# First attention: value matmuls in bursts of four units instead of two, eight probability buffers instead of six, and a shorter scope for a projection table

## The chip, the cores and the metric

The kernel runs on one core of one Trainium2 chip. The metric is the device time of one execution in microseconds; three runs of the kernel before gave 4062.64, 4070.68 and 4073.54 us, a median of 4070.68 us. PE is the matmul engine, DVE VectorE, ACT ScalarE, POOL GpSimd, and SP issues DMAs.

## The reference

The program is a stack of four blocks with a layer norm behind each. Only the first is touched:

```python
q = (x @ Wq.T + bq).reshape(B, T, H, hd)      # B 2, T 2048, H 16, hd 16
k = (x @ Wk.T + bk).reshape(B, T, H, hd)
v = (x @ Wv.T + bv).reshape(B, T, H, hd)
scores = jnp.einsum('bqhd,bkhd->bhqk', q, k) * scale
lag = jnp.abs(idx[:, None] - idx[None, :]).astype(jnp.float32)
scores = scores * jnp.exp(-alpha * lag)
attn = jax.nn.softmax(scores, axis=-1)
out = jnp.einsum('bhqk,bkhd->bqhd', attn, v).reshape(B, T, D)
return out @ Wo.T + bo
```

Behind it come a feed-forward with weights and activations quantized to four bits, a linear attention and a mixture of eight experts.

## The kernel before

**Units and tiles.** The heads are taken two at a time, 16 pairs in all (2 batches times 8). For each pair the scores are computed twice. The first time, 128 "tiles" of 128x512 serve only to find the maximum of every query's row: PE computes a tile into one of three PSUM buffers (`ps_r`, `BANKS = 3`, L623), DVE multiplies it by the decay and takes its maximum in one instruction, followed by a short one that reads the result (both L690), and the buffer is free again. The second time, 64 "units" of 128 keys x 512 queries x 2 heads make the output: PE computes a unit's scores with two matmuls into one of two PSUM buffers (`ps_s`, L645), ACT takes their exp into `prob` (L779), and PE multiplies the probabilities by the values (L661) into `ps_o`. A unit's values are four matmuls in float32, on four strips of 32 columns of the array, which the trace records as eight.

**Diagonal units.** Where keys and queries lie in the same 512 columns (16 of 64 units) the decay can't be folded into the operands. ACT copies such scores to `tb` (L769), POOL multiplies by the decay and subtracts the maxima (L737, L740), and ACT takes the exp from there (L776). `SCORE_ORDER` and `EXP_ORDER` say in which order the 16 units of a block of 512 queries are scored and exponentiated; a diagonal unit's exp comes several units after its copy.

**Order of the work.** It is written out by hand in `body_steps`. A body runs a pair's 64 units beside the tiles of the pair behind it (102 of them, and the first 26 of the one after), two tiles to a unit. `values` steps are put behind every second unit, and cover the two units that lie `LAG` = 4 back. Once in 16 units a `sum` step transposes the finished output (L668), which ACT has moved from `ps_o` to `ot` before (L756, behind the second exp of the next block, when the last values of the block are done), and DVE divides by the sums (L718, L720). The last pair's body has no tiles; the one before it has 102. The middle bodies stand in a loop of two pairs per turn.

**Waits.** PE's tile waits for `ring_free`, which DVE raises when it has read the tile that was in the buffer; its score n waits until ACT has read n-2; its values wait for the exps. An exp n waits for `value`, that is until the values of the unit that last used the same of the `RING` = 6 probability buffers are computed. `PV0` is the count from which `value` starts, one below `RING`.

**The projection table.** `grow` (4 KB a partition), `nalpha`, `alpha` and three bias columns are written by `stage_tables` and read by `stage_project`, both of which are over when `stage_attention` opens; they are held in SBUF until the attention ends.

Of the kernel before, what the change touches and what calls it, by code (L numbers as in the profile page):

```python
# [14 lines left out]
P = 128  # L15
B, T, D = 2, 2048, 256
N = B * T
KC = D // P
NT = N // P
TB = T // P  # L20
# [3 lines left out]
CH = 512  # L24
QB = T // CH
# [32 lines left out]
def up_to(n):  # L58

    return n + 1  # L60
# [257 lines left out]
UNITS = QB * TB  # L318
# [4 lines left out]
TURN = 3  # L323
BANKS = 3
EARLY = 3
RING = 6
LAG = 4
EXP0, PV0, EV0 = TB, 5, 1

# [45 lines left out]
@lru_cache(None)  # L377
def body_steps(kind):

    fold, turn = [("fold", None, 1)], [("turn", None, 1)]
    if kind == "first":
        small = [("tile", t, 1) for t in range(TILES)] + fold + [("tile", t, 2) for t in range(TURN)] + turn
        small += [("tile", t, 2) for t in range(TURN, SKEW)]
        steps, slot = [], 0
        for what, n, ahead in small:
            steps.append((what, n, slot if what != "fold" else None, ahead))
            slot += what != "fold"
        return steps  # L390
    small = []
    if kind != "last":
        small = [("tile", t, 1) for t in range(SKEW, TILES)] + fold
        if kind in ("lead", "mid"):
            small += [("tile", t, 2) for t in range(TURN)] + turn + [("tile", t, 2) for t in range(TURN, SKEW)]
        else:
            small += turn
    steps, done, slot = [], 0, 0
    def next_small(upto):
        nonlocal done, slot  # L400
        while done < min(len(small), upto):
            what, n, ahead = small[done]
            steps.append((what, n, slot if what != "fold" else None, ahead))
            done, slot = done + 1, slot + (what != "fold")

    for two in range(0, UNITS + (LAG if kind == "last" else 0), 2):
        for u in (two, two + 1):
            next_small(EARLY + 2 * u)
            if u < UNITS:
                steps.append(("score", u, None, 0))  # L410
            next_small(EARLY + 2 * u + 1)
        if two >= LAG:
            steps.append(("values", two - LAG, None, 0))
        elif kind != "lead":
            steps.append(("values", UNITS + two - LAG, None, -1))
        if two % TB == TB // 2 and (two > TB or kind != "lead"):
            steps.append(("sum", two // TB - 1 if two > TB else QB - 1, slot, 0 if two > TB else -1))
            slot += 1
    assert done == len(small)
    if kind == "last":  # L420
        steps.append(("sum", QB - 1, slot, 0))
    return steps
# [30 lines left out]
def stage_attention(nc, g, a):  # L453
    with ExitStack() as ctx:
# [61 lines left out]
        with nc.Block() as block:  # L516
# [89 lines left out]
            @block.tensor  # L606
            def _(pe):
                def body(_, this, nxt):
                    for kind, n, slot, ahead in body_steps(body_kind(this, nxt)):
                        whose = (this or nxt.plus(-1)).plus(ahead)  # L610
                        if slot is not None:
                            bank, back = ring_use(body_kind(this, nxt))[slot]
                            at_slot = first_slot(this) + slot
                            if this or slot >= BANKS:

                                pe.wait_ge(s["ring_free"], up_to(at_slot - back + 1))
                        if kind == "tile":
                            hh, rest = divmod(n, TB * QB)
                            qt, kc = divmod(rest, QB)
                            if n == 0:  # L620
                                pe.wait_ge(s[f"p1load{whose.par}"], up_to(whose.half() * 192 + 192))
                            buf = p1[whose.par]
                            pe.matmul(ps_r[:, bank, :], buf[:, hh, 0, qt * P:(qt + 1) * P],  # L623
                                      buf[:, hh, 1, kc * CH:(kc + 1) * CH], start=True, stop=True)\
                              .then_inc(s["ring_full"], 1)
                        elif kind == "turn":
                            pe.wait_ge(s["mred"], up_to(nxt.times(1) + 1))
                            pe.transpose(ps_r[0:2 * TB, bank, 0:P], nm[:], ident[:]).then_inc(s["ring_full"], 1)
                        elif kind == "score":
                            qb, kb, diag = s_unit(n)  # L630
                            if n == 0:
                                pe.wait_ge(s[f"p2load{this.par}"], up_to(this.half() * 288 + 288))
                            if n == 1:
                                pe.wait_ge(s[f"mload{this.par}"], up_to(this.half() * 128 + 128))
                            if SCORE_ORDER[(n - 2) % TB] == "d":

                                pe.wait_ge(s["copied"], up_to(this.times(TB) + diag_count(n - 2) + 1))
                            else:

                                pe.wait_ge(s["exp"], up_to(this.times(UNITS) + place_in(SCORE_ORDER, n - 2, EXP_ORDER) + 1 + EXP0))  # L640
                            buf = p2[this.par]
                            rows = ROWS if diag else ROWS + AUG
                            var = RAW if diag else LEFT if kb < TPC * qb else RIGHT
                            for hh in range(2):
                                mm = pe.matmul(ps_s[:, n % 2, hh, :], buf[0:rows, hh, KEY, kb * P:(kb + 1) * P],  # L645
                                               buf[0:rows, hh, var, qb * CH:(qb + 1) * CH], start=True, stop=True)
                            mm.then_inc(s["score"], 1)
                        elif kind == "values":
                            if n == 0:
                                pe.wait_ge(s[f"vload{whose.par}"], up_to(whose.half() * 16 + 16))  # L650
                            if n % TB == 0:

                                pe.wait_ge(s["evac"], up_to(whose.times(QB) + n // TB + EV0))
                            pe.wait_ge(s["exp"], up_to(whose.times(UNITS) + n + 2 + EXP0))
                            for m in (n, n + 1):
                                qb, kb, _ = e_unit(m)
                                for f in range(2):
                                    for hh in range(2):
                                        q = 2 * f + hh
                                        out = ps_o[32 * q:32 * q + VW, qb % 2, :]  # L660
                                        mm = pe.matmul(out.rearrange("p (j c) -> p j c", c=P), vp[whose.par][:, kb, hh, :],  # L661
                                                       prob[:, m % RING, hh, :].rearrange("p (j f c) -> p f j c", f=2, c=P)[:, f],
                                                       start=(m % TB == 0), stop=(m % TB == TB - 1), skip_group_check=True)
                                mm.then_inc(s["value"], 1)
                        elif kind == "sum":
                            pe.wait_ge(s["evac"], up_to(whose.times(QB) + n + 1 + EV0))
                            for j in range(2):
                                mm = pe.transpose(ps_r[:, bank, j * P:(j + 1) * P], ot[:, j * P:(j + 1) * P], ident[:])  # L668
                            mm.then_inc(s["ring_full"], 1)

                walk(body)(pe)
# [74 lines left out]
            def _(act):  # L746
                def body(_, this, nxt):
# [11 lines left out]
                    for n in range(UNITS):  # L759
# [8 lines left out]
                                act.wait_ge(s["exp"], up_to(this.times(UNITS) + place_in(SCORE_ORDER, mine - 1, EXP_ORDER) - TB + 1 + EXP0))  # L768
                                act.activation(tb[:, k % DIAGS], ps_s[:, (mine - 1) % 2], ACT.Copy).then_inc(s["copied"], 1)  # L769

                        last = UNITS % RING if n < UNITS % RING else RING
                        act.wait_ge(s["value"], up_to(this.times(UNITS) + n - last + 1 + PV0))
                        if diag:
                            k = e_diags.index(n)
                            act.wait_ge(s["less"], up_to(this.times(TB) + k + 1))
# [1397 lines left out]
def post_ln_stack(nc, inputs, out):  # L2173
# [3 lines left out]
    with ExitStack() as ctx:  # L2177
        g = {}

        def sbuf(where, name, shape, dt=F32):  # L2180
            g[name] = where.enter_context(nc.sbuf_tensor(name, shape, dt))
# [14 lines left out]
        sbuf(ctx, "ident", [P, P])  # L2196
        with ExitStack() as attention:
            sbuf(attention, "toep", [P, TOEP])
            sbuf(attention, "grow", [P, 2, CH])
            sbuf(attention, "csc", [P, QB * TB])  # L2200
            sbuf(attention, "nalpha", [P, 1])
            sbuf(attention, "alpha", [P, 1])
            for n in ("bq", "bk", "bq4"):
                sbuf(attention, n, [P, KC])
            stage_tables(nc, g, a)
            stage_project(nc, g, a)
            stage_attention(nc, g, a)
        sbuf(ctx, "logit", [P, NT, E])
        sbuf(ctx, "gate", [P, 2, NT])
# [50 lines left out]
```

## Time and profile before

| | us |
|---|---|
| median of three runs | 4070.68 (4062.64 to 4073.54) |
| the profiled execution, its own time | 4065.74 |
| its span | 4064.2 |
| PE busy | 3197.6 (79%) |
| DVE busy | 2557.4 (63%) |
| ACT busy | 1755.8 (43%) |
| POOL busy | 1472.8 (36%) |

The shares are averages over stages with different limits. The first attention lies between about 300 and 1953 us of the span. Times of rows are counted from the span's start. A row of the timeline gives the start, how long it lasted, the engine, the line and what was computed, merged over instructions of one kind that follow one another (x16), and in brackets an idle stretch before it with what ended it. A matmul's time in a row includes the way through the array; how fast matmuls follow one another is read from their starts.

### The profile page before, as it was taken

What the parts mean: (1) busy time and instruction counts of PE and PEld (TensorE: products, weight loads), DVE (VectorE), ACT (ScalarE), POOL (GpSimd) and SP (SyncE); (2) the same over time, 40 slices, a digit from 0 to 9 for tenths busy, and PEclk for the clock granted to TensorE, in tenths of its full rate; (3) what the DMA queues carried; (4) which work ended last, traced back from release to release, by engine and by line L of the source; (5) the groups of instructions that cost most, each with busy time, mean ns of one, the idle gap of its engine ahead of it and who ended that gap; (6) DMA issues with size and microseconds to landing.
All of it is one profiled execution on the core that took longest, in us unless ns stands there. A gap on an engine that the chain in (4) does not pass through costs nothing. (4 is left out here: it accounts for less than half of the span.)

```text
span 4064.2 us, 72075 instructions
## 1 busy us (share of the span) xinstructions
PE 3197.6 (79%) x21589; PEld 1637.2 (40%) x21590; DVE 2557.4 (63%) x6592; ACT 1755.8 (43%) x2093; POOL 1472.8 (36%) x811
## 2 busy tenths in 40 slices
PE   5539999999999989998335887788887339999970
PEld 2202333333333333332123454455565216666650
DVE  6739998989898989991476777354444302222226
ACT  3302887878787878889211222111211102222210
POOL 2212777777777777778100000000000230000016
PEclk8756999999999999999667999899997569999985
DMA  4743333333333333330230000110001550000014
GB/s 112 216 113 75 82 84 81 75 82 76 81 76 80 77 80 77 79 62 26 50 61 16 11 15 0 71 41 29 25 22 78 206 201 31 31 31 31 31 47 143
DMA packets 200466, 285.30 MB, mean 70 GB/s; under 512 B 91760, under 2 KB 156272, under 8 KB 197840
## 3 DMA queue, kind: packets, MB, share of 16 engines
q1 hardware_dynamic: 185968, 234.81, 23.0%
q0 software_dynamic: 13312, 43.30, 3.0%
q8 instruction: 172, 2.82, 0.3%
q10 hardware_dynamic: 864, 3.15, 0.2%
q14 instruction: 150, 1.23, 0.1%
HBM read 185.37 MB, written 79.00 MB: 65 GB/s over the span
## 5 line engine op out<-in xcount | busy, mean ns | idle before, releaser
L690 DVE CUSTOM_DVE_ANT_0 ps_r<-ps_r,toep 128x512 f32<-128x512 f32 x2048 | 1356.2, 717 | 194.8 <-PE ps_r L623 137.6
L779 ACT ACTIVATE prob<-ps_s,csc 128x1024 f32<-128x1024 f32 x768 | 836.7, 1119 | 185.1 <-PE ps_s L645 134.6
L623 PE MATMUL ps_r<-p 96*128 96x512 bf16 x2048 | 746.4, 403 | 130.9 <-DMA p<-scr_scratch 78.7
L737 POOL TENSOR_TENSOR tb<-tb,toep 128x1024 f32<-128x1024 f32 x256 | 606.1, 2367 | 484.7 <-ACT tb L769 336.6
L645 PE MATMUL ps_s<-p 120*128 120x512 bf16 (+1 forms) x2048 | 618.2, 384 | 41.9 <-ACT tb L769 26.6
L740 POOL TENSOR_TENSOR tb<-tb,mb 128x1024 f32<-128x1024 f32 x256 | 605.6, 2366 | 20.1
L661 PE MATMUL ps_o<-prob,vp 128*32 128x256 f32 x8192 | 553.1, 388 | 1.0 <-ACT prob L779 1.0
L623 PEld LDWEIGHTS ps_r<-p 96*128 96x128 bf16 x2048 | 199.1, 98 | 601.5 <-DVE mp L690 323.8
L769 ACT ACTIVATE tb<-ps_s 128x1024 f32<-128x1024 f32 x256 | 263.0, 1027 | 202.2 <-PE ps_s L645 202.1
L661 PEld LDWEIGHTS ps_o<-prob,vp 128*32 128x32 f32 x8192 | 214.8, 109 | 280.1 <-issue 190.7
L645 PEld LDWEIGHTS ps_s<-p 120*128 120x128 bf16 (+1 forms) x2048 | 181.6, 99 | 273.2 <-ACT prob L779 70.5
L690 DVE DVE_READ_ACCUMULATOR2_ANT mp<- 128x1 f32 x2048 | 290.4, 142 | 0.0
L2014 PE MATMUL ps_ed<-moe_w,e_aT 128*128 x1152 | 267.5, 385 | 16.9 <-ACT e_aT L2034 16.9
L2034 ACT ACTIVATE e_aT<-ps_et 128x512 f32<-128x512 f32 x144 | 78.2, 595 | 461.7 <-PE ps_et L2006 461.7
L776 ACT ACTIVATE prob<-tb 128x1024 f32<-128x1024 f32 x256 | 270.9, 1058 | 3.6 <-POOL tb L740 3.6
L1986 PE MATMUL ps_eu<-moe_w,e_hT 128*128 x584 | 267.1, 601 | 3.1 <-DVE e_hT L2050 3.1
L2014 PEld LDWEIGHTS ps_ed<-moe_w,e_aT 128*128 128x128 f32 x1152 | 212.9, 190 | 59.6 <-issue 33.6
L2059 DVE TENSOR_TENSOR e_u<-ps_eu,moe_b 128x1024 f32<-128x1024 f32 x73 | 89.4, 1225 | 225.5 <-PE ps_eu L1986 225.5
L2103 POOL MEMSET c_acc<- 1x1 f32 x1 | 0.1, 88 | 630.1 <-POOLq L48 630.1
L2073 DVE TENSOR_TENSOR e_y<-ps_ed,moe_b 128x256 f32<-128x256 f32 x72 | 30.6, 425 | 229.5 <-PE ps_ed L2014 229.5
L1127 PE MATMUL ps_u<-wgu,xs 128*128 128x512 f32 (+1 forms) x384 | 161.6, 571 | 6.9 <-DMA xs<-xqT 6.9
L1986 PEld LDWEIGHTS ps_eu<-moe_w,e_hT 128*128 128x128 f32 x584 | 112.4, 193 | 114.9 <-issue 111.3
(289 smaller groups left out, 3540.2 us busy)
## 6 DMA issues: line engine op xcount, KB each, us to landing
p<-scr_scratch SPq DMA_DIRECT2D x288, 192.0 KB
mb<-mrow_scratch SPq DMA_DIRECT2D x16, 2048.0 KB, 7.1
scr_scratch<-part SPq DMA_DIRECT2D x64, 384.0 KB, 6.1
moe_w<-in_W_dram SPq DMA_DIRECT2D x16, 1024.0 KB
p<-scr_scratch SPq DMA_DIRECT2D x96, 128.0 KB
slots_scratch<-l_zero POOLq DMA_DIRECT2D x16, 592.0 KB, 5.2
e_xs<-slots_scratch SPq DMA_DIRECT2D x74, 128.0 KB, 2.0
yslots_scratch<-e_y SPq DMA_DIRECT2D x72, 128.0 KB, 1.7
```

The source lines that it names most:

```text
L623: pe.matmul(ps_r[:, bank, :], buf[:, hh, 0, qt * P:(qt + 1) * P], buf[:, hh, 1, kc * CH:(kc + 1) * CH], start=True, stop=True)\
L645: mm = pe.matmul(ps_s[:, n % 2, hh, :], buf[0:rows, hh, KEY, kb * P:(kb + 1) * P], buf[0:rows, hh, var, qb * CH:(qb + 1) * CH], start=True ...
L661: mm = pe.matmul(out.rearrange("p (j c) -> p j c", c=P), vp[whose.par][:, kb, hh, :], prob[:, m % RING, hh, :].rearrange("p (j f c) -> p f ...
L690: dve.tensor_tensor_reduce(ps_r[:, bank, :], ps_r[:, bank, :], toep[:, col:col + CH], 1.0, -3.0e38, ALU.mult, ALU.max, mp[:, whose.par, hh ...
L737: pool.tensor_tensor(tb[:, k % DIAGS], tb[:, k % DIAGS], toep[:, col:col + CH].unsqueeze(1) .broadcast_to([P, 2, CH]), ALU.mult).then_inc( ...
L740: pool.tensor_tensor(tb[:, k % DIAGS], tb[:, k % DIAGS], mb[:, this.par, :, qb * CH:(qb + 1) * CH], ALU.add).then_inc(s["less"], 1)
L769: act.activation(tb[:, k % DIAGS], ps_s[:, (mine - 1) % 2], ACT.Copy).then_inc(s["copied"], 1)
L776: act.activation(prob[:, n % RING], tb[:, k % DIAGS], ACT.Exp).then_inc(s["exp"], 1)
L779: act.activation(prob[:, n % RING], ps_s[:, mine % 2], ACT.Exp, scale=csc[:, qb * TB + kb:qb * TB + kb + 1]).then_inc(s["exp"], 1)
L1127: mm = pe.matmul(ps_u[t % 2][:, lo:hi], xs[:, par, kc, t * P:(t + 1) * P], g["wgu"][:, kc, lo:hi], start=(kc == 0), stop=(kc == KC - 1), s ...
L1986: mm = pe.matmul(ps_u[:, tile.par, half * CH:(half + 1) * CH], hT[:, kc, :], w["w1"][:, bass.ds(e, 1), kc, half * CH:(half + 1) * CH] .rea ...
L2014: mm = pe.matmul(ps_d[:, 0:D], aT[:, f, :], w["w2"][:, bass.ds(e, 1), f, :].rearrange("p a n -> p (a n)"), start=(f == 0), stop=(f == FK - 1))
```

## The change

Three edits. `BURST = 4` is new: `values` steps come behind every fourth unit and cover the four units that lie four back, and PE's wait and loop over the units of a step (in `stage_attention`) follow. `RING` goes from 6 to 8 and `PV0` from 5 to 7; 64 is a multiple of 8, so the case for a ring that doesn't divide the units is gone. The tables of the projection move into a scope `early` that closes before the attention.

```diff
-RING = 6
+RING = 8
+BURST = 4
 LAG = 4
-EXP0, PV0, EV0 = TB, 5, 1
+EXP0, PV0, EV0 = TB, 7, 1
...
-    for two in range(0, UNITS + (LAG if kind == "last" else 0), 2):
-        for u in (two, two + 1):
+    for four in range(0, UNITS + (LAG if kind == "last" else 0), BURST):
+        for u in range(four, four + BURST):
             next_small(EARLY + 2 * u)
             if u < UNITS:
                 steps.append(("score", u, None, 0))
             next_small(EARLY + 2 * u + 1)
-        if two >= LAG:
-            steps.append(("values", two - LAG, None, 0))
+        if four >= LAG:
+            steps.append(("values", four - LAG, None, 0))
         elif kind != "lead":
-            steps.append(("values", UNITS + two - LAG, None, -1))
-        if two % TB == TB // 2 and (two > TB or kind != "lead"):
-            steps.append(("sum", two // TB - 1 if two > TB else QB - 1, slot, 0 if two > TB else -1))
+            steps.append(("values", UNITS + four - LAG, None, -1))
+        if four % TB == TB // 2 and (four > TB or kind != "lead"):
+            steps.append(("sum", four // TB - 1 if four > TB else QB - 1, slot, 0 if four > TB else -1))
             slot += 1
...
-                            pe.wait_ge(s["exp"], up_to(whose.times(UNITS) + n + 2 + EXP0))
-                            for m in (n, n + 1):
+                            pe.wait_ge(s["exp"], up_to(whose.times(UNITS) + n + BURST + EXP0))
+                            for m in range(n, n + BURST):
...
-                        last = UNITS % RING if n < UNITS % RING else RING
-                        act.wait_ge(s["value"], up_to(this.times(UNITS) + n - last + 1 + PV0))
+                        act.wait_ge(s["value"], up_to(this.times(UNITS) + n - RING + 1 + PV0))
...
-            sbuf(attention, "grow", [P, 2, CH])
             sbuf(attention, "csc", [P, QB * TB])
-            sbuf(attention, "nalpha", [P, 1])
-            sbuf(attention, "alpha", [P, 1])
-            for n in ("bq", "bk", "bq4"):
-                sbuf(attention, n, [P, KC])
-            stage_tables(nc, g, a)
-            stage_project(nc, g, a)
+            with ExitStack() as early:
+                sbuf(early, "grow", [P, 2, CH])
+                sbuf(early, "nalpha", [P, 1])
+                sbuf(early, "alpha", [P, 1])
+                for n in ("bq", "bk", "bq4"):
+                    sbuf(early, n, [P, KC])
+                stage_tables(nc, g, a)
+                stage_project(nc, g, a)
             stage_attention(nc, g, a)
```

How the instructions of PE move, in the middle of a body. Before, with `ps_r` a tile, `ps_s` a score and `ps_o` values:

```order
L661 MATMUL ps_o<-prob,vp 32x256 x8
L623 MATMUL ps_r<-p_1 128x512
L645 MATMUL ps_s<-p_0 128x512 x2
L623 MATMUL ps_r<-p_1 128x512 x2
L645 MATMUL ps_s<-p_0 128x512 x2
L623 MATMUL ps_r<-p_1 128x512
L661 MATMUL ps_o<-prob,vp 32x256 x8
L668 MATMUL ps_r<-ident,ot 128x128 x2
L623 MATMUL ps_r<-p_1 128x512
```

The same place on PE in the changed kernel, one line further down in the file:

```order
L662 MATMUL ps_o<-prob,vp 32x256 x16
L624 MATMUL ps_r<-p_1 128x512
L646 MATMUL ps_s<-p_0 128x512 x2
L624 MATMUL ps_r<-p_1 128x512 x2
L646 MATMUL ps_s<-p_0 128x512 x2
L624 MATMUL ps_r<-p_1 128x512 x2
L646 MATMUL ps_s<-p_0 128x512 x2
L624 MATMUL ps_r<-p_1 128x512 x2
L646 MATMUL ps_s<-p_0 128x512 x2
L624 MATMUL ps_r<-p_1 128x512
L662 MATMUL ps_o<-prob,vp 32x256 x16
```

Eight tiles and eight score matmuls stand between two bursts, in the order that they had, and a burst has sixteen value matmuls in place of eight. A `sum` follows every fourth burst in place of every eighth. The order of ACT's, DVE's, POOL's and SP's work is the same; what an exp waits for on ACT changes.

## Rows read from the trace of the kernel before

**Rows 1.** The page's 40 slices: busy tenths and PE's granted clock.

```profile
PE   5539999999999989998335887788887339999970
DVE  6739998989898989991476777354444302222226
PEclk8756999999999999999667999899997569999985
```

**Rows 2.** The page's groups: count, busy us and mean ns, idle time before.

```profile
L690 DVE CUSTOM_DVE_ANT_0 ps_r<-ps_r,toep 128x512 f32<-128x512 f32 x2048 | 1356.2, 717 | 194.8 <-PE ps_r L623 137.6
...
L737 POOL TENSOR_TENSOR tb<-tb,toep 128x1024 f32<-128x1024 f32 x256 | 606.1, 2367 | 484.7 <-ACT tb L769 336.6
...
L661 PE MATMUL ps_o<-prob,vp 128*32 128x256 f32 x8192 | 553.1, 388 | 1.0 <-ACT prob L779 1.0
```

**Rows 3.** Timeline of PE, mid-stage: start, length, engine, line, operation.

```profile
1007.76 1.07 PE L661 MATMUL ps_o<-prob,vp 128*32 128x256 f32 x16
1008.76 0.39 PE L623 MATMUL ps_r<-p 96*128 96x512 bf16 x1
1008.99 0.60 PE L645 MATMUL ps_s<-p 120*128 120x512 bf16 x2
1009.42 0.60 PE L623 MATMUL ps_r<-p 96*128 96x512 bf16 x2
1009.86 0.60 PE L645 MATMUL ps_s<-p 120*128 120x512 bf16 x2
1010.29 0.38 PE L623 MATMUL ps_r<-p 96*128 96x512 bf16 x1
1010.60 1.07 PE L661 MATMUL ps_o<-prob,vp 128*32 128x256 f32 x16
```

**Rows 4.** Timeline of DVE, the same stretch.

```profile
1009.34 0.70 DVE L690 CUSTOM_DVE_ANT_0 ps_r<-ps_r,toep 128x512 f32<-128x512 f32 x1
...
1009.99 0.70 DVE L690 CUSTOM_DVE_ANT_0 ps_r<-ps_r,toep 128x512 f32<-128x512 f32 x1
```

**Rows 5.** Timeline of DVE and PE before the first units, where DVE is slower.

```profile
344.73 0.73 DVE L690 CUSTOM_DVE_ANT_0 ps_r<-ps_r,toep 128x512 f32<-128x512 f32 x1
...
345.57 0.61 PE L623 MATMUL ps_r<-p 96*128 96x512 bf16 x1
```

**Rows 6.** Timeline of PE, end of the last pair.

```profile
1928.74 1.94 PE L661 MATMUL ps_o<-prob,vp 128*32 128x256 f32 x16
...
1948.25 1.93 PE L661 MATMUL ps_o<-prob,vp 128*32 128x256 f32 x32
```

**Rows 7.** Timeline of ACT mid-stage, and of PE where it waits for ACT.

```profile
1009.62 1.11 ACT L779 ACTIVATE prob<-ps_s,csc 128x1024 f32<-128x1024 f32 x1 [0.72 <-PE ps_s L645]
...
1020.50 0.38 ACT L756 ACTIVATE ot<-ps_o 128x256 f32<-128x256 f32 x1 [1.07 <-PE ps_o L661]
1020.78 1.02 ACT L769 ACTIVATE tb<-ps_s 128x1024 f32<-128x1024 f32 x1
1021.68 2.12 ACT L779 ACTIVATE prob<-ps_s,csc 128x1024 f32<-128x1024 f32 x2
...
1058.79 2.11 ACT L779 ACTIVATE prob<-ps_s,csc 128x1024 f32<-128x1024 f32 x2
...
1059.95 0.61 PE L645 MATMUL ps_s<-p 120*128 120x512 bf16 x2
```

**Rows 8.** Timeline of PE, four of the sum steps.

```profile
1005.41 0.44 PE L668 MATMUL ps_r<-ident,ot 128*128 128x128 f32 x2
...
1029.29 0.44 PE L668 MATMUL ps_r<-ident,ot 128*128 128x128 f32 x2
...
1851.14 0.44 PE L668 MATMUL ps_r<-ident,ot 128*128 128x128 f32 x2
...
1873.22 0.44 PE L668 MATMUL ps_r<-ident,ot 128*128 128x128 f32 x2
```

**Rows 9.** Engines by stretch: busy us of each, granted clock, DMA.

```profile
1880.00:1900.00 20.00, 16.48 (x161) 5.37 (x162) 0.50 (x2) 18.43 (x20) 16.62 (x8) 1.00 0.00 1
```

## The prediction

> **What bounds the kernel now.** I read the page's slices first, then its costliest groups, then the timeline of one engine at a time inside the first attention. In the slices [rows 1] that stage fills the third to the eighteenth or nineteenth of 40: PE and DVE both stand at 9 tenths there, with PE's clock at full. The groups [rows 2] say what this work is: 2048 "tiles" (a 128x512 matmul on PE, then the multiply-and-maximum on DVE, L690), and 8192 value records on PE, 8 for each of 1024 units (16 pairs of heads times 64 units). Two engines at 9 tenths can't be ranked by shares, so I turn to the order within one period.
>
> The period of PE is two units long [rows 3]: a value burst of 16 records (L661), one tile, one score (two matmuls), two tiles, one score, one tile, next burst. It takes 1010.60 - 1007.76 = 2.84 us and nothing in it waits: burst start to next matmul 1.00, tile to score 0.23, score to tile 0.43, two tiles 0.44, score 0.43, last tile to burst 0.31. DVE [rows 4] takes a tile every 1009.99 - 1009.34 = 0.65 us, so four cost 2.60, and it is idle for the other 0.24 us of the period: the first tile behind the burst starts on PE at 1008.76, on DVE at 1009.34, 0.58 later. So PE is the bound, but by 0.24 us in 2.84 only, and DVE's idle time is the shadow of the burst. Two couplings matter now. Tiles go through three PSUM buffers: where DVE is the slower one, PE's next matmul into a buffer starts 345.57 - 344.73 = 0.84 us after DVE began with what was in it [rows 5]. Scores go through two: PE's score n waits until ACT has read n-2.
>
> **The change, part by part.** *Fewer, longer bursts.* The tiles and scores keep their order; two bursts become one of 32 records. The trace has one such burst, at the end of the last pair [rows 6]: 32 records in 1.93 us, where 16 take 1.07 [rows 3]. The next matmul starts 0.07 before the end, so 1.86 after the start. A pair of short bursts costs 2 x (1.00 + 0.31) = 2.62, the long one 1.86 + 0.31 and an ordinary tile-to-tile step of 0.22 in place of the second tile-to-burst step: 2.39. PE's own work per four units falls from 5.68 to 5.45 us. If PE alone decided, that would be 0.23 x 256 = 59 us gained.
>
> *What is late next: DVE, through the three buffers.* I call the eight tiles of four units a to h, and put the start of a on PE at 0. PE: a 0, score 0.23, b 0.66, c 0.88, score 1.09, d 1.53. DVE: a 0.58, then one every 0.65: b 1.23, c 1.88, d 2.53, e 3.18, f 3.83, g 4.48, h 5.13, done at 5.78. Tile e needs b's buffer, free at 1.23 + 0.84 = 2.07, so PE waits 0.33 there (e 2.07, score 2.29, f 2.72); g needs d's, 2.53 + 0.84 = 3.37, another 0.43 (g 3.37, score 3.59); h 4.02, just as e's buffer comes free. The burst starts at 4.33 and the next a at 4.33 + 1.86 = 6.19. DVE sees it at 6.77, and has been idle since 5.78. So the period is 6.19 us: DVE's work 8 x 0.65 = 5.20, and 0.99 idle. This doesn't hang on the details: when the burst starts, h must be out, so e must have been read, so from DVE's start on e it has four tiles, 2.60 us, before it, while 0.84 + 0.31 = 1.15 go by until the burst, 1.86 in it and 0.58 behind it: 3.59 - 2.60 = 0.99. The same walk gives 2.84 for the kernel before. The loss per four units is 6.19 - 5.68 = 0.51 us.
>
> *ACT.* It is fed by two score buffers and by the diagonal units that come back from POOL (two passes of 2.37 us each, [rows 2]). From [rows 7]: an exp every 1.00 us, a copy 0.90 (1020.78 to 1021.68), an evacuation 0.28, a score's first matmul to ACT's start 0.63 (1008.99 [rows 3] to 1009.62), ACT's start to the score that waits for it 1.16 (1058.79 to 1059.95). Walked along sixteen units (twelve exps of 1.00, four from tb which I take as 0.95, four copies of 0.90, 0.28: 19.7 us of work), ACT empties both buffers in every burst, and three of PE's scores come late. After the burst at a block's start the evacuation has to wait for all of it; the copy behind it starts 0.5 late and holds back the second score by 0.48, of which DVE's queue absorbs all but 0.06. The fourth score of the third group waits 0.31 for a copy, that of the fourth group 0.39 for an exp, and each puts off the burst by as much. Together 0.76 us in sixteen units. The price from below is 0 (hidden by DVE's own lateness); from above it is as much again, 1.5, if a late exp also makes POOL's results late. I take the walk's 0.76.
>
> *Sixteen units.* Now they take 1029.29 - 1005.41 = 23.88 us from one "sum" step to the next [rows 8]: 8 x 2.84 = 22.72, the sum itself about 0.5, and 0.66 of waits for ACT. After: 4 x 6.19 = 24.76, the sum 0.5, ACT's 0.76: 26.02. The loss is 2.14 us. The bounds are 24.76 + 0.5 = 25.26 (loss 1.4) and 26.8 (loss 2.9).
>
> *How often.* Tiles run beside the units in 14 pairs of 128 tiles and one of 102: 237 groups of eight, 59 times sixteen units. 59 x 2.14 = 126 us, bounds 82 and 172.
>
> *The rest of the stage.* The last fourteen units of the fifteenth pair and all of the last have no tiles: about five times sixteen units, 1873.22 - 1851.14 = 22.1 us each [rows 8], with ACT as the bound. There ACT gets 19.7 us of work and idles in each long burst while two scores last 2.0 us at most: about 1.6, 0.2, 1.3 and 0.1 us in the four groups, 22.9 in all. That is 0.8 x 5, about 4 us; below, 0, and above, 10.
>
> *Eight probability buffers.* Exp n now waits for the values of n-8. The burst before has always delivered those, as it did with six and short bursts, so I give the wait nothing, in either direction. Without the two added buffers ACT would hang on the long burst; with them it only runs out of scores.
>
> *The table's scope.* No instruction is added, and every consumer of these tensors is over before the attention opens; only addresses move. Nothing, and at most a microsecond either way. The waits of POOL, SP and the loads name the same events; the loads have a whole pair to arrive.
>
> *Sum.* 4065.74 (the profiled execution) + 126 + 4 = 4196; the bounds 4065.74 + 82 = 4148 and 4065.74 + 172 + 10 = 4248. The median of the runs, 4070.7, lies 5 us above that execution, within their spread of 11 us, so I leave the forecast at 4197.
>
> **A rule weighed.** The row shows a wait-free PE period and full clock [rows 1, 3]. The Trainium skill (TensorE: Matmul & The Clock Gate, "Loop structure matters more than you think") advises keeping matmuls back to back, which the long burst does; its Part 2, on what each phase is for, says that only weight loads are pulled ahead and matmuls stay in order, so no later tile can slip into the burst. By the first alone the change would gain the 59 us of the rival below; the second leaves DVE's 0.99 us standing. No run yet shows which prevails.
>
> **The rivals.** *PE alone decides* (faster). If the buffers held enough for DVE to bridge the long burst, the period would be 5.45 us and the time 4065.7 - 59 = 4007, or up to 4053 if ACT's lateness takes most of it. For it: PE is the bound today. Against it: already now DVE idles 0.24 us in each short burst, and what stands in the buffers is 2.60 us of work (e to h) against 1.15 + 1.86 + 0.58 = 3.59.
>
> *The two cancel* (within 0.3%): DVE would have to idle only 0.48 us per long burst, half of what the buffers allow. I see nothing in the rows for it.
>
> *The clock falls.* PE now waits in small pieces in every group. At half clock 16 records take 1.94 us in place of 1.07 [rows 6], and PE's 5.45 us become up to 10.9. If one group in twenty ran so, 12 x 5 = 60 us would come on top: 4257. Against it: from 1880 to 1900 us PE waits up to 1.5 us for ACT, and the clock granted is 1.00 [rows 9]. The Trainium skill names the case (same page, "A second HAM failure mode: psum-queue depth-cycling"): small idle stretches between groups of matmuls can make the clock swing. By it this rival would hold; the row speaks against it.
>
> *ACT and POOL add up.* The late copies make POOL's passes (4.7 us, four in sixteen units, 19 of 26) late in turn, and exps from tb wait. It decides from the point where a copy comes over 1 us late; then 1.5 us more in sixteen units, 59 x 1.5 = 88: 4285.
>
> **How the numbers follow.** The forecast's mechanism with its bounds has 0.84, PE alone 0.05, cancelling 0.03, the clock 0.04, ACT and POOL 0.04. The range 4155 to 4240 leaves out the faster cases and half of the two slow ones, and a little of the walk's own bounds. Slower by over 0.3% (about what a measurement of this kernel can tell from no change, 12 us): 0.84 + 0.04 + 0.04 = 0.92; the same 0.03; faster 0.05.
>
> **What would show it.** After: a period of PE of about 6.2 us with 32 value records in one burst; DVE idle about 1.0 us once per burst, waiting for PE; two waits of PE's tiles for DVE in each group, 0.3 to 0.4 us; DVE's share in the stage down from 9 to about 8 tenths; sums 26 us apart; the evacuation waiting over 2 us; full clock. I am wrong if DVE bridges the burst, if 32 records in mid-stage take other than 1.93 us, or if ACT's waits turn out longer than DVE's.

## The result and the profile after

The changed kernel takes 4204.88 us (median of four runs, 4202.96 to 4206.98) against 4072.11 for the kernel before (median of four as well): ratio 1.0324, 95% interval 1.0296 to 1.0353. Its profiled span is 4201.9 us, 137.7 us over the one before.

The slices and groups of the page after, which answer to [rows 1, 2]:

```profile
DVE  6749887878787878886067677444545402222226
PEclk9757999999999999999956899899999559999995
...
L691 DVE CUSTOM_DVE_ANT_0 ps_r<-ps_r,toep 128x512 f32<-128x512 f32 x2048 | 1344.5, 724 | 286.9 <-PE ps_r L624 271.5
...
L662 PE MATMUL ps_o<-prob,vp 128*32 128x256 f32 x8192 | 496.5, 383 | 0.5 <-ACT prob L779 0.5
```

In the stage DVE's tenths alternate between 7 and 8, and the clock's stay at 9, as before. The value matmuls are the same 8192 records; they are busy 57 us less, since 256 times one row of 1.93 us stands in place of two of 1.07. DVE's tiles cost the same to 1%, but wait 271.5 us for PE's tiles instead of 137.6. PE mid-stage, one whole period (columns as in [rows 3]):

```profile
1028.50 1.93 PE L662 MATMUL ps_o<-prob,vp 128*32 128x256 f32 x32
1030.37 0.39 PE L624 MATMUL ps_r<-p 96*128 96x512 bf16 x1
1030.59 0.60 PE L646 MATMUL ps_s<-p 120*128 120x512 bf16 x2
1031.03 0.60 PE L624 MATMUL ps_r<-p 96*128 96x512 bf16 x2
1031.46 0.59 PE L646 MATMUL ps_s<-p 96*128 96x512 bf16 x2
1031.89 0.91 PE L624 MATMUL ps_r<-p 96*128 96x512 bf16 x2
1032.64 0.60 PE L646 MATMUL ps_s<-p 120*128 120x512 bf16 x2
1033.07 0.38 PE L624 MATMUL ps_r<-p 96*128 96x512 bf16 x1
1033.71 0.39 PE L624 MATMUL ps_r<-p 96*128 96x512 bf16 x1 [0.26 <-DVE mp L691]
1034.26 0.61 PE L646 MATMUL ps_s<-p 120*128 120x512 bf16 x2 [0.16 <-ACT tb L770]
1034.70 0.38 PE L624 MATMUL ps_r<-p 96*128 96x512 bf16 x1
1035.01 1.93 PE L662 MATMUL ps_o<-prob,vp 128*32 128x256 f32 x32
```

The burst takes 1.93 us and gives PE back after 1.87. The fifth tile is late (two tiles take 0.91 us where two without a wait take 0.60), the seventh waits for DVE, and here the fourth score waits for ACT, so this period is 6.51 us; the one ahead of it, from 1022.27, is 6.23. A period in which no score is late for ACT takes 1073.83 - 1067.65 = 6.18:

```profile
1067.65 1.93 PE L662 MATMUL ps_o<-prob,vp 128*32 128x256 f32 x32
...
1073.83 1.93 PE L662 MATMUL ps_o<-prob,vp 128*32 128x256 f32 x32
```

DVE and ACT:

```profile
1029.28 0.73 DVE L691 CUSTOM_DVE_ANT_0 ps_r<-ps_r,toep 128x512 f32<-128x512 f32 x1
1030.94 0.70 DVE L691 CUSTOM_DVE_ANT_0 ps_r<-ps_r,toep 128x512 f32<-128x512 f32 x1 [0.88 <-PE ps_r L624]
...
1024.35 0.38 ACT L757 ACTIVATE ot<-ps_o 128x256 f32<-128x256 f32 x1 [2.37 <-PE ps_o L662]
...
1031.23 1.11 ACT L779 ACTIVATE prob<-ps_s,csc 128x1024 f32<-128x1024 f32 x1 [0.70 <-PE ps_s L646]
...
1038.00 1.11 ACT L779 ACTIVATE prob<-ps_s,csc 128x1024 f32<-128x1024 f32 x1 [1.79 <-PE ps_s L646]
```

DVE could go on at 1029.28 + 0.65 and starts at 1030.94: 1.01 us idle in this burst and in one more of the four between two sums, 1.2 to 1.3 us in the other two. ACT waits too, up to 2.4 us. Sum steps, to be set beside [rows 8]:

```profile
1036.88 0.44 PE L669 MATMUL ps_r<-ident,ot 128*128 128x128 f32 x2
...
1062.66 0.44 PE L669 MATMUL ps_r<-ident,ot 128*128 128x128 f32 x2
```

Sixteen units take 25.78 us, 1.90 more than the 23.88 before. Taken over a whole pair (from the same timelines) it is 25.78 + 25.79 + 26.14 + 27.08 = 104.8 against 23.88 + 23.88 + 23.60 + 24.78 = 96.1, so 2.16 per sixteen units.

### The profile page after: what moved, and what is told of

Same layout as the page of the kernel before. It is cut to its first block and busy times, and to the rows that moved or that the text cites. A ratio compares the mean times of both kernels' runs of the same rounds, so it can differ in the third digit from the quotient of the medians.

```text
span 4201.9 us, 72057 instructions
## 1 busy us (share of the span) xinstructions
PE 3217.0 (77%) x21589; PEld 1665.4 (40%) x21590; DVE 2532.8 (60%) x6592; ACT 1751.4 (42%) x2093; POOL 1473.9 (35%) x811
## 3 DMA queue, kind: packets, MB, share of 16 engines
q1 hardware_dynamic: 185968, 234.81, 22.1%
q14 instruction: 150, 1.23, 0.1%
## 5 line engine op out<-in xcount | busy, mean ns | idle before, releaser
L691 DVE CUSTOM_DVE_ANT_0 ps_r<-ps_r,toep 128x512 f32<-128x512 f32 x2048 | 1344.5, 724 | 286.9 <-PE ps_r L624 271.5
L624 PE MATMUL ps_r<-p 96*128 96x512 bf16 x2048 | 775.7, 405 | 217.2 <-DMA p<-scr_scratch 76.6
L662 PE MATMUL ps_o<-prob,vp 128*32 128x256 f32 x8192 | 496.5, 383 | 0.5 <-ACT prob L779 0.5
L662 PEld LDWEIGHTS ps_o<-prob,vp 128*32 128x32 f32 x8192 | 240.7, 110 | 222.5 <-issue 79.6
```

Source lines behind the costliest of these rows:

```text
L691: dve.tensor_tensor_reduce(ps_r[:, bank, :], ps_r[:, bank, :], toep[:, col:col + CH], 1.0, -3.0e38, ALU.mult, ALU.max, mp[:, whose.par, hh ...
```

## The experiments

In the table stands the distance of two sum steps inside a pair ("sixteen units"), read from each kernel's timeline of PE; ratios are against the kernel before, run beside each of them (medians of 4065.0 to 4072.5 us). A "light" engine leaves out a part of its work, and with it of the result; which part is said below.

| kernel | time, us | ratio (interval) | sixteen units, us |
|---|---|---|---|
| before | 4072.11 | 1 | 23.88 |
| changed | 4204.88 | 1.0324 (1.0296 to 1.0353) | 25.78 |
| bursts of 2, rest of the change kept | 4064.91 | 1.0001 (0.9986 to 1.0016) | 23.87 |
| bursts of 4, evacuation later | 4200.01 | 1.0328 (1.0295 to 1.0361) | 25.72 |
| bursts of 1 | 4118.23 | 1.0126 (1.0096 to 1.0156) | 25.17 |
| bursts of 2, two tile buffers | 4313.98 | 1.0609 (1.0576 to 1.0642) | 27.35 |
| bursts of 4, light DVE | 4152.70 | 1.0203 (1.0181 to 1.0225) | 25.31 |
| bursts of 2, light DVE | 4032.68 | 0.9915 (0.9892 to 0.9938) | 23.63 |
| bursts of 4, light ACT | 4151.77 | 1.0211 (1.0189 to 1.0233) | 25.15 |
| bursts of 4, both light | 4037.21 | 0.9913 (0.9897 to 0.9929) | 23.39 |
| bursts of 2, both light | 4034.72 | 0.9915 (0.9899 to 0.9930) | 23.46 |
| before, evacuation later | 4069.40 | 0.9994 (0.9981 to 1.0006) | 23.92 |
| before, copy ahead of evacuation | 4047.40 | 0.9944 (0.9931 to 0.9958) | 23.39 |

**Which edit costs.**

```diff
-BURST = 4
+BURST = 2
```

> The changed kernel with bursts of two units again; the eight probability buffers and the table's scope stay. Theory (the long burst drains the three tile buffers and leaves DVE idle): all of the loss comes from the burst, so this is the kernel before again, 4060 to 4078 us, sums 23.9 us apart. Rival (the eight buffers or the moved addresses cost something): it stays near 4205 us, or a part of the 133 us stays.

4064.91 us beside 4065.0 for the kernel before. With bursts of two the eight buffers and the moved table together are worth nothing either way; the loss is the burst's. (The kernel with bursts of four and six buffers wasn't tried: by the hand-written order ACT would wait for values that PE computes only behind a score that waits for ACT.)

**What stands in the buffers decides.** The kernel before, with fewer tile buffers:

```diff
-BANKS = 3
+BANKS = 2
...
-    users = [-3, -2, -1]
+    users = [-2, -1]
...
-        if kind != "lead" and what == "sum" and n in (0, QB - 1):
+        if kind != "lead" and what == "sum" and n == 0:
```

(The two lower edits keep each pair's tiles starting in the same buffer.)

> The kernel before, bursts of two units, with two PSUM buffers for the tiles instead of three. Theory (what DVE has before it when a burst begins decides): PE's third tile waits for 0.58 + 0.84 = 1.42, the fourth for 2.08, the burst starts at 2.39 and the period is 3.39 us instead of 2.84; 59 x 8 x 0.55 = 260 us more, 4300 to 4350 us, DVE idle about 0.8 us at each burst. Rival (PE's own work or ACT's scores set the period, tile buffers have slack): 4070 to 4090 us.

4313.98 us. DVE and PE, in the profile of this kernel:

```profile
1002.24 0.70 DVE L690 CUSTOM_DVE_ANT_0 ps_r<-ps_r,toep 128x512 f32<-128x512 f32 x1
1002.86 0.14 DVE L690 DVE_READ_ACCUMULATOR2_ANT mp<- 128x1 f32 x1
1003.56 0.70 DVE L690 CUSTOM_DVE_ANT_0 ps_r<-ps_r,toep 128x512 f32<-128x512 f32 x1 [0.56 <-PE ps_r L623]
...
1001.98 1.07 PE L661 MATMUL ps_o<-prob,vp 128*32 128x256 f32 x16
...
1004.38 0.39 PE L623 MATMUL ps_r<-p 96*128 96x512 bf16 x1 [0.36 <-DVE mp L690]
...
1005.36 1.07 PE L661 MATMUL ps_o<-prob,vp 128*32 128x256 f32 x16
```

The period is 3.38 us, walked beforehand as 3.39: a short burst drains two buffers much as a long one drains three.

**The other direction.** `BURST = 1` in the changed kernel:

> The changed kernel with bursts of one unit. Theory: DVE is bridged with ease, PE is the bound and pays one more turn of 0.24 us in two units, a period of 3.05 to 3.08 us instead of 2.84; ACT's waits of 0.66 in sixteen units shrink. 59 x (8 x 0.22 less 0.3) = 86 us over the kernel before, 4150 to 4180 us. Rival (only PE's absence from tiles and scores costs, turns between kinds of matmul are nearly free): 4072 us or less.

4118.23 us, 32 below the expected range, and the rival is wrong too. Two units take 3.08 us, as worked out:

```profile
1001.97 0.64 PE L662 MATMUL ps_o<-prob,vp 128*32 128x256 f32 x8
...
1005.05 0.64 PE L662 MATMUL ps_o<-prob,vp 128*32 128x256 f32 x8
```

8 x 3.08 + 0.5 = 25.1: all of PE's waits for ACT are gone, about 0.6 us and not the 0.3 that I allowed, and a pair takes 25.17 + 25.17 + 24.60 + 25.67 = 100.6 us, only 4.5 above the kernel before. The turns of the loop are shorter too (below). So going over to the value matmuls and back costs 3.08 - 2.84 = 0.24 us; with bursts of one unit this outweighs the waits that are saved, with bursts of four the drained consumers outweigh what is saved of it.

**Is ACT's wait beside DVE's?** `if n % TB == 1` in front of the evacuation becomes `== 2`, in the changed kernel:

> The changed kernel, with ACT's evacuation of the finished output behind the third exp of a block instead of the second, so that ACT no longer waits 2.37 us in the long burst for it. Theory: ACT's wait lies beside DVE's idle time, so it is worth at most the 0.06 us by which the second burst of a block comes late: 4195 to 4208 us. Rival (ACT's waits set the period): 1 to 2.4 us are gained in each of 59 blocks of sixteen units, 4065 to 4145 us.

4200.01 us, 25.72 in sixteen units, 0.06 less. But ACT only waits elsewhere, so this says less than I had expected:

```profile
1022.67 1.11 ACT L779 ACTIVATE prob<-ps_s,csc 128x1024 f32<-128x1024 f32 x1 [1.80 <-PE ps_s L646]
1023.69 0.38 ACT L757 ACTIVATE ot<-ps_o 128x256 f32<-128x256 f32 x1
```

The evacuation waits no longer, the exp ahead of it waits 1.80 us for a score: with two score buffers ACT is drained by the burst whatever it does first.

**DVE relieved.** In three of four tiles DVE takes half of the columns, so the maxima leave out the keys that are far away:

```diff
-dve.tensor_tensor_reduce(ps_r[:, bank, :], ps_r[:, bank, :], toep[:, col:col + CH],
+lo, hi = (0, CH) if kc == qt // TPC else (CH // 2, CH) if kc < qt // TPC else (0, CH // 2)
+dve.tensor_tensor_reduce(ps_r[:, bank, lo:hi], ps_r[:, bank, lo:hi], toep[:, col + lo:col + hi],
...
```

> The changed kernel (bursts of four, three tile buffers), with less for DVE to do: in three of four tiles it takes only the 256 columns nearer to the diagonal, so the maximum leaves out keys over 256 away. PE's matmuls are the same. Theory (DVE, drained in the long burst, is the bound): DVE's eight tiles fall from 5.20 to about 3.6 us, its idle time no longer matters, and PE's 5.45 us a group with ACT's waits decide: 22.8 to 23.4 us in sixteen units instead of 25.8, 30 to 60 us below the same edit with bursts of two, 3990 to 4025 us. Rival (ACT or PE's turns set the period of the changed kernel): it keeps most of its time, 4150 to 4190 us, and stays above the bursts of two.

> The same lighter work of DVE with bursts of two units. Theory: PE sets the period of 2.84 us already, so the units take 23.9 us in sixteen as before; only the tiles ahead of the first unit, where DVE is alone the bound, get 10 to 20 us shorter: 4040 to 4060 us. Rival (DVE's 0.65 us a tile is the true bound of the kernel before): 2.60 or less in two units, 3950 us or less.

Bursts of two: 4032.68 us, some 7 below the range; sixteen units are 0.25 us shorter, since PE's first tile behind a sum no longer waits for DVE. Bursts of four: 4152.70, and there the expectation fails by 130 us; the time lies in the range of the rival, and above that of the bursts of two. PE's tiles wait little, and yet sixteen units take 25.31 us. PE, and ACT beside it:

```profile
1025.88 0.60 PE L624 MATMUL ps_r<-p 96*128 96x512 bf16 x2
1027.29 0.60 PE L646 MATMUL ps_s<-p 120*128 120x512 bf16 x2 [0.82 <-ACT tb L771]
...
1024.27 1.11 ACT L780 ACTIVATE prob<-ps_s,csc 128x1024 f32<-128x1024 f32 x1 [0.67 <-PE ps_s L646]
1025.28 1.05 ACT L777 ACTIVATE prob<-tb 128x1024 f32<-128x1024 f32 x1
1026.22 1.01 ACT L771 ACTIVATE tb<-ps_s 128x1024 f32<-128x1024 f32 x1
1027.13 2.12 ACT L780 ACTIVATE prob<-ps_s,csc 128x1024 f32<-128x1024 f32 x2
1031.04 1.11 ACT L780 ACTIVATE prob<-ps_s,csc 128x1024 f32<-128x1024 f32 x1 [1.79 <-PE ps_s L646]
```

ACT's rows show waits of 0.67, 1.79, 0.66 and 1.94 us in the four bursts of sixteen units. Counted from where it could have gone on (an exp's row lasts 1.11 us, but the next one can start after 1.00) they are 0.82, 1.91, 0.78 and 2.10: 5.6 in all, and with its 19.7 of work 25.3. And PE's scores are the ones that start late, for ACT (the table below). The theory that DVE alone is the bound had fallen; the second says that both consumers are drained, each through its own buffers, and that either alone holds the period.

**ACT relieved, and both.** Each exp in the changed kernel, from the scores and from `tb`, takes half of the queries, and leaves the others' probabilities at one:

```diff
...
-act.activation(prob[:, n % RING], ps_s[:, mine % 2], ACT.Exp,
+act.activation(prob[:, n % RING, :, 0:CH // 2], ps_s[:, mine % 2, :, 0:CH // 2], ACT.Exp,
...
```

> The changed kernel (bursts of four), with less for ACT to do: each exp takes 256 of the 512 queries of a unit and leaves the others' probabilities out (set to one once); DVE, POOL and PE are unchanged. First theory (DVE alone is drained by the long burst) and second theory (DVE and ACT are both drained, each through its own buffers, and either alone holds the long period) expect the same here: DVE's walk of 4 x 6.19 + 0.5 = 25.3 us in sixteen units instead of 25.8, 4130 to 4165 us with the last pair shorter. Third theory (ACT alone is drained and DVE's idle time only follows): PE's 22.3 us, 3950 to 4010 us.

> The changed kernel with both, DVE's lighter tiles and ACT's half exps. Second theory: with neither consumer near its limit only PE's own work is left, 4 x 5.45 + 0.3 to 0.5 = 22.1 to 22.4 us in sixteen units, and the long burst shows its gain of 0.24 us per four units: 3900 to 3950 us, below the same kernel with bursts of two. If something else in the long burst costs (the clock, the score's order, instruction issue), the sixteen units stay above 23 us and it is not below it.

> The same two lighter consumers with bursts of two units: PE's 8 x 2.84 + 0.3 = 23.0 us in sixteen units, 3945 to 3990 us. The difference to the bursts of four is PE's saving alone, 59 x 0.7 to 0.9 = 40 to 55 us.

ACT relieved alone: 4151.77 us and 25.15 in sixteen units, DVE's walk of 25.3 to within 0.15. That excludes the third theory, ACT alone. DVE's row is again the one of the changed kernel:

```profile
1009.59 0.70 DVE L693 CUSTOM_DVE_ANT_0 ps_r<-ps_r,toep 128x512 f32<-128x512 f32 x1 [0.87 <-PE ps_r L626]
```

Both relieved: 23.39 us. So of the 2.4 us that the two together hold, relieving one gives back 0.5 or 0.6. But both kernels with two light consumers miss their ranges, bursts of four by 87 us and bursts of two by 45: over sixteen units the long burst is only 0.07 us ahead (23.39 against 23.46), not the 0.7 to 0.9 expected, and over a whole pair it isn't ahead at all (94.4 against 94.3). PE's rows say why. Here is a period of 5.66 us with bursts of four; two of its tiles start late for DVE, by 0.05 and 0.16 us (a row of two tiles that lasts 0.76 in place of 0.60), and 5.45 is left:

```profile
1008.28 1.93 PE L664 MATMUL ps_o<-prob,vp 128*32 128x256 f32 x32
...
1012.60 0.76 PE L626 MATMUL ps_r<-p 96*128 96x512 bf16 x2
...
1013.94 1.93 PE L664 MATMUL ps_o<-prob,vp 128*32 128x256 f32 x32
```

The same can be added up for sixteen units of every kernel: how much later each tile and each score starts than the step from the matmul ahead of it takes where nothing waits (0.22 us between tiles and scores, 0.31 from a burst), and for whom it waited:

| kernel | sixteen units, us | tiles late for DVE | scores late for ACT | the rest |
|---|---|---|---|---|
| before | 23.88 | 0.24 | 0.62 | 23.0 |
| changed | 25.78 | 2.45 | 1.23 | 22.1 |
| bursts of 4, light DVE | 25.31 | 0.6 to 0.8 | 2.4 to 2.6 | 22.1 |
| bursts of 4, light ACT | 25.15 | 2.58 | 0.47 | 22.1 |
| bursts of 4, both light | 23.39 | 0.6 to 0.8 | 0.5 to 0.7 | 22.1 |
| bursts of 2, both light | 23.46 | 0 | 0.47 | 23.0 |
| bursts of 1 | 25.17 | 0.23 | 0 | 24.9 |

The rest is PE's own work. It is 0.9 us shorter with bursts of four than with bursts of two in every kernel, as 4 x 0.235 says; the lateness eats it up. Neither relief is complete: with DVE light some lateness is still DVE's, with ACT light some is still ACT's. With both consumers light 0.6 to 0.8 us of it go to DVE, which is late even with its lighter tiles, and both burst lengths lose about 0.5 us to ACT's copy behind the evacuation. (In the profiled executions the turns of the loop took some 20 us more with bursts of four, but the medians of the two kernels lie only 2.5 us apart.)

**A version that beats both.** The copy that stands behind the evacuation costs the kernel before 0.48 us of PE in sixteen units. First its evacuation one exp later, as above:

> The kernel before with ACT's evacuation behind the third exp of a block instead of the second. There PE's second score after the burst waits 0.31 to 0.48 us in sixteen units for the copy that stands behind the evacuation, and PE is the bound. Theory: that wait goes, 0.3 to 0.5 us in each of 60 blocks, 4035 to 4050 us. Rival (DVE's slack of 0.24 us a burst or another wait takes its place): within 5 us of the kernel before.

4069.40 us, no gain, as the rival had it. PE's wait has moved to the next block's first values, which may not be written before the old ones are read:

```profile
1020.89 1.07 PE L661 MATMUL ps_o<-prob,vp 128*32 128x256 f32 x16 [0.45 <-ACT ot L756]
```

Then between the copy and the exp:

```diff
                                 act.activation(tb[:, k % DIAGS], ps_s[:, (mine - 1) % 2], ACT.Copy).then_inc(s["copied"], 1)
+                            if n % TB == 2 and (n > TB or this.back()):
+                                evacuate(n // TB - 1)
...
-                        if n % TB == 1 and (n > TB or this.back()):
-                            evacuate(n // TB - 1)
```

> The kernel before, with the evacuation put between the next diagonal copy and the third exp: the copy (whose score is there) runs beside the burst, PE's second score behind it is no longer late, and the evacuation still comes before PE's next block of values needs it. Theory: the 0.48 us that PE loses in sixteen units goes and nothing replaces it, 60 x 0.3 to 0.5 = 18 to 29 us, 4035 to 4050 us. Rival (another wait takes its place, as it did with the evacuation behind the third exp): within 5 us of the kernel before.

```profile
1007.53 1.02 ACT L769 ACTIVATE tb<-ps_s 128x1024 f32<-128x1024 f32 x1
1008.70 0.38 ACT L756 ACTIVATE ot<-ps_o 128x256 f32<-128x256 f32 x1 [0.16 <-PE ps_o L661]
```

4047.40 us, ratio 0.9944 (0.9931 to 0.9958): 23.39 us in sixteen units, 0.49 less. It is the fastest kernel of the study that computes all of the result. With bursts of four this order wasn't tried.

## Why the prediction was right, and where its reasons were not

**PE's saving.** 32 records in 1.93 us mid-stage, as at the end of the last pair [rows 6]: right, and the 0.9 us in sixteen units are there in every kernel with bursts of four. The rival "PE alone decides" is excluded; it doesn't come about even with both consumers light.

**DVE, drained through three buffers.** The period without a late score takes 6.18 us of the 6.19 walked; DVE's idle time of 0.99 us is 1.01 in two bursts of four; the waits of two tiles are there; the same walk with two buffers (3.39) met 3.38. Right as a mechanism and in size: with ACT's exps halved sixteen units take 25.15 of the 25.26 forecast without ACT, 0.47 of them still for ACT's copy.

**ACT.** Here the reasoning was incomplete. I priced ACT's lateness as 0.76 us on top of DVE's, and took ACT for the smaller of the two. The walk behind that figure ran both at once, so the total came out (26.02 against 25.78, 0.24 too long), but its parts did not: PE's tiles are late for DVE by 2.45 us in sixteen units, where the walk has 4 x 0.76 = 3.04, and its scores for ACT by 1.23, where it has 0.76. And it hid that ACT's own chain is as long as DVE's: with DVE light it is 25.31. The step that failed is not in the sum but in the words "what is late next: DVE". In the expectation for light DVE the same step cost 130 us, since I there added 0.76 to PE's work without walking ACT anew.

**ACT and POOL add up.** This rival is excluded: in the page after, the exps from `tb` have no idle time before them, where they waited 3.6 us for POOL in the page before.

```profile
L776 ACT ACTIVATE prob<-tb 128x1024 f32<-128x1024 f32 x256 | 270.7, 1058 | 0.0
```

**How often, and the rest.** 59 x 2.14 = 126 us was forecast. The 2.14 is right by luck: the walk was 0.24 too long, and two of the four distances of a pair, which no walk covered, lose 2.3 to 2.5 us and not 1.90, which brings the mean to 2.16. Of the 137.7 us between the spans, 3.2 are lost before the first sum, 110.6 in the 52 distances between sums that have tiles and no turn of the loop (2.13 each), 17.7 in the five that have a turn, and 6.9 in the six at the end, without tiles (130.8 us against 123.9), where 4 were forecast; 0.7 come back behind the stage. Not in the sum at all were the turns of the loop: a distance across a turn was 35.2 us and is 38.7 (means of five), 3.5 more, which makes 7 us over five turns beyond 2.14 each.

**Eight buffers, the table's scope, the clock.** Nothing, nothing, and as before: right, the first two shown together by the bursts of two. PE's late starts in every group, 3.7 us of 25.78, did not bring the clock down (9 tenths in the stage's slices, before and after); it falls at the turns of the loop, before and after alike (last section).

## What to carry to other kernels

Before a burst on one engine is made longer, compare its length, plus the way to each consumer, with the work that the consumer's buffers hold when it begins; do this for every consumer, each with the others out of the picture. A walk with all of them at once can give the right time and the wrong bound: two chains of nearly equal length look like one with a small addition, and relieving either alone gives back a fifth or a quarter (0.5 or 0.6 of 2.4 us here). Adding up on the fed engine how late each kind of instruction starts, and for whom, shows both. And an instruction that waits should stand behind the short one that others wait for, as the copy before the evacuation shows.

## What the runs showed of the hardware that I had not expected

At each turn of the loop all engines stop, and the profile shows nothing that the first of them wait for ("issue"). In the kernel before, the rows of PE and DVE behind the last burst of the turn, and two stretches (length, then busy us of PE, PE's weight loads, DVE, ACT and POOL, and behind them the granted clock, here 1.00 and 0.50):

```profile
1060.70 1.07 PE L661 MATMUL ps_o<-prob,vp 128*32 128x256 f32 x16
1065.32 1.46 PE L623 MATMUL ps_r<-p 96*128 96x512 bf16 x3 [3.54 <-issue]
...
1070.28 1.03 PE L623 MATMUL ps_r<-p 96*128 96x512 bf16 x2 [2.66 <-DVE mp L690]
...
1067.97 0.70 DVE L690 CUSTOM_DVE_ANT_0 ps_r<-ps_r,toep 128x512 f32<-128x512 f32 x1 [5.87 <-issue]
...
1060.00:1064.00 4.00, 1.77 (x20) 0.57 (x19) 2.10 (x8) 2.85 (x3) 0.00 (x0) 1.00 0.85 212
...
1068.00:1072.00 4.00, 1.72 (x5) 0.66 (x5) 2.94 (x9) 0.77 (x1) 3.08 (x2) 0.50 1.04 145
```

PE stands idle for 3.54 us, and the clock granted falls to half; two tiles then take 1.03 us in place of 0.60, and from 1076 on the clock is at 1.00 again. That the engines want for instructions there is a guess; no run tests it.

A distance across a turn takes 35.2 us in the kernel before, where the same distance without a turn takes 24.8, so a turn costs 10.4 us. With bursts of one unit it is 8.0 (33.6 less 25.7), in the changed kernel 11.6 (38.7 less 27.1), with both consumers light 11.8 for bursts of two and 16.0 for bursts of four (means of five turns of one execution each). That it grows with the burst was seen, not explained.
